# Router logits with the router weights stationary in four column strips

## The reference, cut to what matters

```python
xf = x.reshape(-1, D)                       # 4096 x 128, after a layer norm
logits = xf @ router_w.T                    # 8 experts
scores = jax.nn.softmax(logits, axis=-1)
topk_scores, topk_ids = jax.lax.top_k(scores, TOP_K)     # TOP_K = 2
topk_scores = topk_scores / topk_scores.sum(-1, keepdims=True)
...
h = jax.nn.silu(xf @ wg) * (xf @ wu)        # per expert
acc = acc + w[:, None] * (h @ wd)
```

## Time and profile before

| | before |
|---|---|
| median of three runs | 1526.19 us |
| the profiled execution: its time | 1528.99 us |
| its span | 1527.3 us |
| TensorE matmul busy | 1166.0 us (76%) |
| VectorE busy | 997.7 us (65%) |
| ScalarE busy | 787.2 us (52%) |
| GpSimd busy | 592.1 us (39%) |
| TensorE's granted clock, mean | 0.876 |

### The profile page before, as it was taken

How to read it: one execution, slowest core, us unless ns; L and a number is a source line. 1 busy time by engine, 2 the same in 40 slices (tenths; PEclk the granted TensorE clock), 3 DMA queues, 4 the chain that set the end, 5 groups by cost and what they waited for, 6 DMA issues and landing times.

```text
span 1527.3 us, 34396 instructions
## 1 busy us (share of the span) xinstructions
PE 1166.0 (76%) x11393; PEld 901.6 (59%) x11394; DVE 997.7 (65%) x1974; ACT 787.2 (52%) x1333; POOL 592.1 (39%) x859
## 2 busy tenths in 40 slices
PE   0577559999984776549999914899998654999991
PEld 0355336666652555539999912455554353999991
DVE  5799769898955998573333356888997357333333
ACT  0444216555663443236666661567666523666666
POOL 2122122121200222016676723566766301667671
PEclk9999659999997998559999966899999855999996
DMA  8000023322210000101111133343243010111115
GB/s 255 19 1 0 1 49 58 53 55 55 51 24 1 1 0 1 55 9 46 47 48 46 47 123 56 58 78 65 56 83 58 2 56 9 46 47 48 47 47 178
DMA packets 161960, 75.58 MB, mean 49 GB/s; under 512 B 126540, under 2 KB 153941, under 8 KB 161877
## 3 DMA queue, kind: packets, MB, share of 16 engines
q1 hardware_dynamic: 152404, 55.06, 16.4%
q0 software_dynamic: 9472, 19.42, 4.3%
HBM read 28.69 MB, written 15.86 MB: 29 GB/s over the span
## 4 chain that ended last, share of the span: by engine, by line
PE 53%; DVE 24%; issue 7%; ACT 6%; DMA 3%; POOL 3%; SPq 2%; DVEq 1%; POOLq 0%; ACTq 0%
PE PS L990 17%; PE PS L1010 8%; PE PS L656 4%; PE PS L358 3%; DVE sg L790 2%; PE PS L638 2%; PE PS L622 2%; PE PS L575 2%; DVE m L790 2%; PE PS L950 2%; PE PS L610 1%; ACT pt L1070 1%; SPq L882 1%; DVE q_amax L266 1%; DMA qT<-qs 1%
## 5 line engine op out<-in xcount | busy, mean ns | idle before, releaser
L990 PE MATMUL PS<-xTs,pt 128*128 128x128 f32 x2336 | 287.7, 277 | 0.0
L715 ACT ACTIVATE pt<-PS 128x768 f32<-128x768 f32 (+1 forms) x256 | 227.6, 917 | 111.2 <-PE PS L638 59.4
L990 PEld LDWEIGHTS PS<-xTs,pt 128*128 128x128 f32 x2336 | 276.0, 194 | 0.0
L1114 DVE TENSOR_TENSOR pt<-pt,PS 128x512 f32<-128x512 f32 x146 | 100.4, 687 | 240.4 <-PE PS L990 210.9
L1227 POOL DMA_INDIRECT xs<-rows,src x152 | 147.3, 969 | 193.3 <-DVE src L1108 147.6
L1039 ACT ACTIVATE pt<-wgu 128x1024 f32 x148 | 156.2, 1057 | 93.2 <-issue 84.2
L1236 POOL DMA_INDIRECT outs<-ys,dst x144 | 142.0, 986 | 85.6 <-DVE ys L1122 78.5
L790 DVE TENSOR_REDUCE m<-PS 128x4 f32<-128x1024 f32 x128 | 149.2, 1217 | 12.9 <-PE PS L575 12.3
L1010 PE MATMUL PS<-wdn,pt 128*128 x1152 | 152.2, 275 | 0.0
L1010 PEld LDWEIGHTS PS<-wdn,pt 128*128 128x128 f32 x1152 | 140.0, 192 | 0.0
L575 PE MATMUL PS<-tables 64*128 64x128 bf16 (+2 forms) x1536 | 132.0, 251 | 0.0
(11 more groups left out here) (228 smaller groups left out, 2120.2 us busy)
## 6 DMA issues: line engine op xcount, KB each, us to landing
pt<-outs SPq DMA_DIRECT2D x16, 512.0 KB, 5.0
rows<-qT SPq DMA_DIRECT2D x12, 256.0 KB, 2.4
xs<-rows,src POOLq DMA_INDIRECT x152, 2.5
outs<-ys,dst POOLq DMA_INDIRECT x144, 2.3
wgu<-in_L_ffn_w_gate SPq DMA_DIRECT2D x1, 2048.0 KB
wgu<-in_L_ffn_w_up SPq DMA_DIRECT2D x1, 2048.0 KB
wdn<-in_L_ffn_w_down SPq DMA_DIRECT2D x8, 256.0 KB
qT<-hqT SPq DMA_DIRECT2D x128, 4.0 KB
```

Of the source, the lines that this page charges most:

```text
L715: s.activation(k.pt[:, a % 4, :, 0:w], k.PS[:, self.bank:self.bank + 2, 0:w], ACT.Exp, scale=self.scale).then_inc(self.s_p, 1)
L990: last = t.matmul(k.PS[:, 1 + 2 * p + w, c * P:(c + 1) * P], k.wst[:, 1 - p, w, c * P:(c + 1) * P], k.xTs[:, p, :], start=True, stop=True)
L1114: v.tensor_tensor(k.hs[:, p, :], k.sgs[:, p, :], k.PS[:, 2 + 2 * p, :], ALU.mult).then_inc(self.s_h, 1)
```

## The change

The logits are now made with the router weights stationary, and transposed.

- `rw` becomes 32 columns wide (8 of weights, 24 of zeros; GpSimd clears it at the start, SyncE loads the 8).
- Half the tokens are one round `r` of four groups. For a round, `logits(r)` issues four matmuls (L951 of the changed kernel): `rw` stationary in column strip `u` of the array, group `u` of transposed tokens moving with 512 columns, output in partitions 32u to 32u+31 of bank 5 + r.
- ScalarE copies that bank to `lgT` (L1032), which lies in the part 3 of `pt`.
- `back(r)` transposes `lgT` in four pieces (L957) into bank 4 or 7, where each token's 8 logits of group `u` stand in columns 32u to 32u+7 of piece `j`.
- VectorE takes the maximum and subtracts it per half (L1161, L1162), with a wait of its own for each.
- TensorE's order is written anew: five groups of transposes, `logits(0)`, three groups of transposes, `back(0)`, `logits(1)`, `back(1)`. ScalarE may overwrite `xnTg` for group 4 and later only after `logits(0)`.

```diff
-        def logits(g):
-            eng.wait_ge(self.s_xnT, g + 1)
+        def logits(r):
+            for u in range(4):
+                eng.wait_ge(self.s_xnT, 4 * r + u + 1)
+                last = t.matmul(k.PS[32 * u:32 * u + 32, 5 + r, :], k.rw[:, :], k.xnTg[u], start=True, stop=True)
+            last.then_inc(self.s_lgT_ps, 1)
+
+        def back(r):
+            eng.wait_ge(self.s_lgT, r + 1)
             for j in range(GT):
-                o = (g * GT + j) * NE
-                last = t.matmul(k.PS[:, 4, o:o + NE], k.xnTg[g % 4][:, j * P:(j + 1) * P], k.rw[:, :],
-                                start=True, stop=True)
+                last = t.transpose(k.PS[:, 4 + 3 * r, j * P:(j + 1) * P], k.lgT[:, r, j * P:(j + 1) * P], k.ident[:, :])
             last.then_inc(self.s_lg_ps, 1)
-        transposes(0)
-        transposes(1)
-        for g in range(NG):
-            if g + 2 < NG:
-                transposes(g + 2)
-            logits(g)
+        for g in range(5):
+            transposes(g)
+        logits(0)
+        for g in range(5, NG):
+            transposes(g)
+        back(0)
+        logits(1)
+        back(1)
...
             if g >= 4:
-                eng.wait_ge(self.s_lg_ps, g - 3)
+                eng.wait_ge(self.s_lgT_ps, 1)
             s.activation(k.xnTg[g % 4], k.PS[:, g % 4, :], ACT.Copy).then_inc(self.s_xnT, 1)
+            if g % 4 == 3:
+                eng.wait_ge(self.s_lgT_ps, g // 4 + 1)
+                s.activation(k.lgT[:, g // 4, :], k.PS[:, 5 + g // 4, :], ACT.Copy).then_inc(self.s_lgT, 1)
...
-        eng.wait_ge(self.s_lg_ps, NG)
...
-        logits = k.PS[:, 4, 0:NT * NE].rearrange("p (t e) -> p t e", e=NE)
-        ch.run(v.tensor_reduce(k.mx[:, :], logits, AX.X, ALU.max))
-        v.tensor_tensor(lg, logits, bc(k.mx[:, :]), ALU.subtract).then_inc(self.s_lg, 1)
+        for r in range(2):
+            half = slice(r * NT // 2, (r + 1) * NT // 2)
+            logits = k.PS[:, 4 + 3 * r, :].rearrange("p (j u e) -> p u j e", j=GT, u=4)[:, :, :, 0:NE]
+            mx = k.mx[:, half].rearrange("p (u j) -> p u j", u=4)
+            eng.wait_ge(self.s_lg_ps, r + 1)
+            ch.run(v.tensor_reduce(mx, logits, AX.X, ALU.max))
+            last = v.tensor_tensor(lg[:, half, :].rearrange("p (u j) e -> p u j e", u=4), logits,
+                                   mx.unsqueeze(3).broadcast_to([P, 4, GT, NE]), ALU.subtract)
+        last.then_inc(self.s_lg, 1)
...
-        self.rw, self.wgu = sb("rw", [P, NE]), sb("wgu", [P, 2, NE, FF])
+        self.rw, self.wgu = sb("rw", [P, 32]), sb("wgu", [P, 2, NE, FF])
...
+        self.lgT = self.pt[:, 3, :, :]
...
-            load(k.rw[:, :], a["router_t"])
+            load(k.rw[:, 0:NE], a["router_t"])
...
             nc.gpsimd.memset(k.wraw[:, :], 0.0).then_inc(s_wz, 1)
+            nc.gpsimd.memset(k.rw[:, :], 0.0)
             nc.gpsimd.memset(k.bload[:, :], 0.0).then_inc(s_bz, 1)
```

More of the change, by code:

```diff
@@ L904, in __init__ @@
         self.s_lg_ps = k.sem(name + "_lg_ps")
+        self.s_lgT_ps = k.sem(name + "_lgT_ps")
+        self.s_lgT = k.sem(name + "_lgT")
         self.s_lg = k.sem(name + "_lg")
```

## The result

| | before | changed |
|---|---|---|
| median of four runs | 1526.47 us (1525.87 to 1528.49) | 1505.0 us (1502.87 to 1508.65) |
| ratio, 95% interval | 1 | 0.9857 (0.9845 to 0.9869) |
| the profiled execution: span | 1527.3 us | 1505.1 us |
| TensorE's granted clock, mean | 0.876 | 0.894 |

The kernel is 21.5 us faster; the forecast was 12.3 us, and 1505.0 lies under its range of 1510.5 to 1518. The direction and the place were right, the size was not.

The account below looks back on a forecast made before the run. It took TensorE's transposes and narrow logits at 1.2 GHz, ahead of the exponential in both expert layers, as the bound. Saving 6.2 us a front, 12.3 in all, from 1526.2 gave 1513.9 us, range 1510.5 to 1518.

Parts of the forecast that it names:

- step 3: First layer's logits(0): four strips at once, so two rounds of 0.88 us, 1.76 us in all, from 620.48 to 622.24.
- The rival that named the clock: Wide matmuls raise TensorE's clock in the front, right behind logits(0): 1.8 us more a layer, 1510.3 us; 9%.
- Steps 1 and 2: Front's start: five transpose groups paced by VectorE, leaving the queue at 620.33, then 0.15 us for the array's shape change.
- the serial rival: In logits, the strips run one after another, 7.04 us a round: 4.4 us slower a layer, 1535 us; 7%.
- Step 4 to 6: Transposes of groups 5 to 7 to 625.03, ScalarE's copies at 0.60 us, logits(1) 626.06 to 627.82, back(1) complete at 629.80.
- Step 7: VectorE's maximum and subtraction on the last half alone: 2 x 0.32 = 0.64 us, at most 0.92; exponential at 630.48.
- Step 8: Table load of 1.28 us ahead of the exponential comes behind ScalarE's last copy, ends at 629.95, hidden by 0.53 us.
- the forecast's balance: Per front: 12.56 us of logits go; strips 3.52, transposes back 1.76 and smaller terms come; 6.2 us saved.
- One strip at a time: The serial rival's case for logits: 7.04 us a round, kernel at 1535 us; 7%.
- two at a time: In logits, only two strips run at once, 3.52 us a round: saves 2.7 us a layer, 1520.8 us; 4%.
- less than fully: In logits, strips overlap three at a time on the mean, 2.35 us a round: saves 5.0 a layer, 1516.2 us; 10%.
- something else ends last: Behind the front, lists or gathers might hang on another queue, so no gain: 1526.2 us; 3%.

Follow-up runs that it names:

- e2: The changed kernel with the old narrow logits of groups 0 to 3 put back as extra work between the first transposes: 1520.41 us, ratio 0.9955.
- e3: The changed kernel with four extra matmuls ahead of logits(0), all writing strip 0 of another bank: 1515.12 us, ratio 0.9924.
- e6: The changed kernel with back(0) behind logits(1), a quarter of the normalising on GpSimd, and filler transposes ahead of front and expert loop: 1504.47 us, ratio 0.9862.
- e8: Label not assigned in the text; the changed kernel with either filler(20) alone ahead of the expert loop (1507.88 us) or group 0's narrow logits put back (1511.21 us).

## Why the prediction was wrong

**What failed** is the clock: every step was priced at 0.50 throughout, as the front before had it. It went to 1.00 ahead of step 3. The rival that named the clock got 9%, and only a gain of 1.8 us a layer: it had the wide matmuls raise it, behind `logits(0)`. No row of before separates the work from the place, and I read 0.50 with TensorE busy for 20.26 of 20.57 us as a property of the place. The order alone and the one group of narrow matmuls put back show that it is the work.

Step by step, in the first front, from the first transpose:

- Steps 1 and 2 (five groups at VectorE's pace, change of shape): `logits(0)` forecast at 5.05 us, measured 4.60, since the last group of transposes already ran at the upper clock (4.6 to 5.1 in the six fronts).
- Step 3, four strips at once: right. Two rounds of 0.45 us at 2.4 GHz, of 0.86 at 1.2 GHz (e2). The waits of their own, which the serial rival built on, cost nothing where the data is there (e2: four starts within 0.03 us). The change of shape is 0.1 us at 2.4 GHz (strip 3 is 0.18 behind the others, so its second pass starts at 619.14 and takes 0.43; the transposes start at 619.67) and 1.87 - 2 x 0.86 = 0.15 at 1.2 GHz (e2), as forecast.
- Step 4 to 6: TensorE no longer decides. The transposes of group 7 start at 7.09 us, when VectorE is done; forecast 8.7 for TensorE's sake. `logits(1)` starts at 8.11, forecast 10.63. It has 1.36 us in the chain, not the 0.90 of two rounds, since its strip 3 starts 0.36 late behind ScalarE's copy of group 7, whose end the weight load waits for:

```profile
622.38 0.14 PEld L951 LDWEIGHTS PS<-wraw,rw 128*32 128x32 f32 x2 [0.22 <-ACT wraw L1029]
```

- Step 7: 0.65 us against 0.64. Eight columns out of 32 cost nothing more.
- Step 8: the cover of 0.53 us over the table load shrank to 0.10: the load ends at 625.36, the exponential starts at 625.46. It is hidden, just.

One reading was off without touching the sum: "some 30 us" for L950 came from a rounded 2%; its pieces in the chain are 5 x 1.51 + 4.93 = 12.5 us a layer, 25 in all.

**The sum.** Forecast 15.05 us a front, measured 11.56 to 11.88 in the three profiles of the changed kernel: 3.2 to 3.5 us too much, twice, is the mis-sized term. The fronts give 2 x 9.5 = 19.1 us. By the forecast's balance, of which e2 bears out the rounds and the change of shape, the new front at 1.2 GHz throughout is worth 12.3 of them, and the clock gave the other 6.8; no run holds the whole new front at 1.2 GHz. The measured 21.5 are 2.4 more than the fronts. That part is open: the second attention was 309.9 to 311.6 us in the three profiles of the changed kernel and 310.4 to 314.1 in the three of before, but in e3, e6 and e8, which have the new order too, it was 312.9 to 313.3, and the interval of the ratio is worth 3.7 us by itself.

**The rivals.** One strip at a time and two at a time are excluded by e2 and e3, "less than fully" by the rounds, "something else ends last" by what follows the front: from the exponential to the gathers' list (L1108, L1118 of the changed kernel) it is 39.24 us before and 39.25 after. The Trainium skill ("TensorE: Matmul & The Clock Gate", section "Why this matters for your kernels") has 3.07 times for four row strips; the column strips here gave 3.8. The drain at a change of tiling mode that the Trainium skill names ("TensorEngine Tiling (Array Packing)", under its key properties) can be no more here than the 0.10 and 0.15 us above.

## What to carry to other kernels

A small product with a wide stationary tile and few moving columns pays for the weight load: here 1.57 / 8 = 0.20 us a pass for 8 columns at 1.2 GHz, where a transpose of 128 took 0.22. Swap the operands, put the narrow one in column strips and transpose the narrow result back. Before pricing work that goes away at the clock of its stretch, ask whether it is that work which keeps the clock there: price the sum at both levels. When a serial engine leaves the chain, look how far its neighbours are behind it: here a quarter of VectorE's work less was worth 0.2 and 0.4 us.

## What the runs showed of the hardware

The granted clock followed the work and not only how busy TensorE was. With 64 narrow passes among its transposes (128 columns loaded, 8 moved) it was 1.2 GHz in all six fronts of the kernel before, TensorE busy for 20.26 of 20.57 us. A row of five groups of plain transposes was followed by 2.4 GHz in every front in which it began at 1.2 GHz, 4.0 to 5.2 us behind its first transpose. And matmuls of different strips did not keep the program's order: in e3, L951's strips 1 to 3 start at 620.04, ahead of the last L963 of strip 0 at 620.47, which the program issues first.
